# Attention in a four-stage kernel: mask products shared by four heads, three probability buffers, the next queries turned in two parts

## The chip, the cores and the metric

The kernel runs on one core of a Trainium2 chip as one program. The metric is the device time of one execution in microseconds. Each core has TensorE (PE, matrix products), VectorE (DVE), ScalarE (ACT), GpSimd (POOL) and SyncE (SP), which here only issues DMAs. Every engine works its instructions off in order and waits on semaphores.

## The reference, cut to what matters

Input `x` and context `ctx_2048` are 8 batches of 256 rows of 512 float32 numbers. Two layers follow, each a gated cross-attention and a gated feed-forward part. The change touches the first attention:

```python
x = x + tanh(g_xattn[0]) * _L0_xattn_ref(_layernorm(x), ctx_2048, mask_SxS2, mask_BxS2, Wq, bq, Wk, bk, Wv, bv, Wo, bo)

# _L0_xattn_ref: H = 32 query heads of HD = 16, G = 8 key/value groups, 4 query heads share a group
q = X @ Wq.T + bq; k = enc @ Wk.T + bk; v = enc @ Wv.T + bv
scores = einsum('bgrqd,bgkd->bgrqk', q, k) / sqrt(16)
scores = where(causal_mask, -inf, scores); scores = where(padding_mask, -inf, scores)
out = einsum('bgrqk,bgkd->bgrqd', softmax(scores), v) @ Wo.T + bo
```

The "causal" mask is one 256 x 256 mask for all heads and batches; the padding mask is one row per batch. Everything is float32; the kernel keeps float32 accuracy with products of float16 high and low parts.

## The kernel before, in words

The kernel has four phases in one program. Phase A is the first attention, phase B the first feed-forward part with ternary weights, phase C the second attention, phase D the second feed-forward part with routing. Phase A is a software pipeline over the batches b = 0 to 7, written out by hand: each engine has a function `body(b, ...)` of NS = 32 steps, and the order of its instructions is the order of these steps. A step n of batch b holds

- `turned_scores(b, n)` on PE: the scores with keys on the partitions, for two heads at once, 512 columns (L748, L750), into one of two banks;
- ScalarE: two exponentials of that bank, one in float16 (`ph`, L1031) and one in float32 (`prob`, L1032);
- POOL: `pl = prob - ph` (L1143), the low half of the probability. `prob` has 2 buffers, `ph` and `pl` have NP = 4;
- `times_v(b, n - LAG)` on PE, LAG = 3 steps later: 12 narrow products with the values (L767, L769, L771);
- `scores(b + 1, n)` on PE: the scores of the next batch with queries on the partitions (L727, L730), of which VectorE takes the row maxima (L1232).

The maxima are needed before the exponentials. They are negated, turned by PE (`turn_maxima`, L738), copied by ScalarE (`take_maxima`, L957) and written by DMA (`place_maxima`, L549) into a spare row of the turned queries `qT`, so that `turned_scores` subtracts them.

A head takes 64 of the 128 rows of a product. A chunk of `qT` stacks two heads (2i, 2i+1). A chain of products goes over these two heads in the same bank: first `half == 0`, a mask product (identity times the added mask, 512 columns, L727 and L748) and the key chunk [k; 0], which gives head 2i. When the bank has been read, `half == 1` adds the key chunk [-k; k], which turns the scores of head 2i into those of head 2i+1. So there is one mask product for every two products of the chain, in steps with n % 4 in (0, 1), and 16 chunks of queries per batch. The queries come into `qT` by DMA transposes from SP (`place_q`, L559), 8 per batch; the keys by PE transposes (`turn_k`, L713) and VectorE copies (L1225).

Other work is spread over the steps: the projections of batch b + 2 (`q_of` in steps 15 to 18 and 21 to 24, `kv_of` in 19, 20, 25 and 26; ScalarE and VectorE take their results in `high_q` L934, `low_q` L1206, `high_kv`, `low_kv`), the output projection of batch b - 1 (transposes L780 in steps 5 and 6, products in steps 7 to 14), the last normalisation of batch b - 1 on VectorE (`normalise`, L1248 and L1251, step 3), the layer-norm moments of batch b + 3 on VectorE (`moments`, L1177 to L1183, step 4, for b up to 4), the normalisation on ScalarE (`normal`, L970, steps 11 and 13), and on POOL the cut of context and input of batch b + 3 into halves (`FRONT`; L1076, L1080 for the context, L1087, L1091 for the input). Context and input go through the same buffers `fbuf` and `fcut`: `normal` writes `fbuf` and first waits for both low halves of the context (`c_lo`). SP loads and places all of these in its own order of the steps.

In batches 4 to 7 the weights of phase B are made ternary on the side: VectorE scales and rounds a piece (`magnitude`, L1194), ScalarE takes its sign (`sign`, L996), SP turns it by DMA. Batch 7 has 14 such pieces, in steps 1, 3, ..., 27, and no scores of a next batch.

Before body 0 stands a stretch in which the scores of batch 0 (32 steps), the projections of batches 0 and 1 and the first transposes are done; there batch 0's queries are turned by PE (`turn_q`, L701).

```python
    LAG = 3
    PQ, PK = (15, 21), (19, 25)
    NEG0, NEG1 = 27, 4
    NORM = LAG + 8
    def which(m):
        u = m % 16
        return u // 8, 4 * (m // 16) + 2 * (u // 4 % 2) + u % 2, u // 2 % 2
```

Of the kernel before, what the change touches and what calls it, by code (L numbers as in the profile page):

```python
# [60 lines left out]
def flamingo(nc, a, out, phases="ABCD"):  # L61
    with ExitStack() as ctx:
# [204 lines left out]
        with nc.Block() as block:  # L267
# [5 lines left out]
            @block.gpsimd  # L273
            def _(pool):
                of_a[1](pool)
                of_b[1](pool)
# [11 lines left out]
            @block.vector  # L288
            def _(dve):
                low_output, residual = of_a[4](dve)  # L290
                of_b[4](dve, low_output, residual)
# [44 lines left out]
def phase_a(nc, a, env):  # L336
# [8 lines left out]
    def sb(name, shape, dt=F32):  # L345
# [5 lines left out]
    XTh = sb("a_xTh", [P, KC, 2, 2 * P], F16)  # L351
    XTl = sb("a_xTl", [P, KC, 2, 2 * P], F16)
# [6 lines left out]
    qk = sb("a_qk", [P, 2, 2, H0 // 2, S], F16)  # L359
    qT, kT = qk[:, :, 0], qk[:, :, 1]  # L360
# [32 lines left out]
    brow = sb("a_brow", [1, NB])  # L393
    blow = sb("a_blow", [1, NB], F16)
# [7 lines left out]
    mx = sb("a_mx", [P, 2, 2, 2, H0 // 4])  # L402
# [7 lines left out]
    on = sb("a_on", [P, 2, 2, D])  # L410
# [4 lines left out]
             "lk0", "lk1", "hv0", "hv1", "lv0", "lv1", "tq", "tq0", "tq1", "tk", "cq", "ck", "S", "M", "nm",  # L415
             "nt", "nc", "ng0", "ng1", "ST", "E", "L", "AV", "ON", "To0", "To1", "hO0", "hO1", "lO0", "lO1", "O0", "O1", "x0", "x1", "ch")
# [6 lines left out]
    o_hi, o_lo, o_tp = (sem("o_" + n) for n in ("hi", "lo", "turned"))  # L423
    n_ch, n_var, n_rstd, n_nm, n_nrm, n_half = (sem("n_" + n) for n in (
        "chain", "var", "rstd", "nmean", "normed", "half"))
# [6 lines left out]
    t_tp = [sem(f"t_turned{i}") for i in range(2)]  # L432

    NS = 2 * G0 * 2
    LAG = 3
# [8 lines left out]
    NEG0, NEG1 = 27, 4  # L444
# [10 lines left out]
    NPIECE = 32  # L455
    ROUND = 12582912.0
    SUM_AT = [1, 5, 9, 13, 17, 21, 25, 29]
    CUT_AT = [1, 6, 11, 17, 23, 28]
    WO_AT = [12, 14, 16, 18]
# [20 lines left out]
    def cut_piece(b, n):  # L480
# [3 lines left out]
        if b == 7 and n in LAST_AT:  # L484
            return 18 + LAST_AT.index(n)

# [21 lines left out]

    def on_sp(sp):
# [8 lines left out]
        def place_ctx(f):  # L518
            if f >= 2:
                sp.wait_ge(ev["KV1"], f - 1)  # L520
            for t in range(2):
# [4 lines left out]
            for t in range(2):  # L526
# [4 lines left out]
        def place_x(f):  # L531
            if f >= 2:
                sp.wait_ge(ev["Q1"], f - 1)
            for t in range(2):
                sp.wait_ge(x_lo, 2 * (f - 1) + t + 1)
                cols = slice(t * P, (t + 1) * P)
                sp.dma_start_transpose(XTh[:, :, f % 2, cols], fcut[:, t, 0, :]).then_inc(x_tp[f % 2], 16)
                sp.dma_start_transpose(XTl[:, :, f % 2, cols], fcut[:, t, 1, :]).then_inc(x_tp[f % 2], 16)

        def load_piece(l):  # L540
            if l >= NST:
# [2305 lines left out]
```

## Time and profile before

| | us |
|---|---|
| median of 3 runs (lowest, highest) | 1677.6 (1674.11, 1680.73) |
| the profiled execution | 1674.66 |
| its span | 1672.9 |
| PE, DVE, ACT, POOL busy in the span | 1577.2, 972.7, 709.0, 824.7 |
| mean granted TensorE clock | 0.984 |

The span goes from the first to the last instruction of the profiled execution. Busy times of PE are those of overlapping products whose ends are modelled. Body 0 starts at 78.5 us, body 1 at 130.4, body 5 at 340.0, body 6 at 390.7 and body 7 at 441.3 (the first L750 of each); the attention's last exponential is at 491.6.

### The profile page before, as it was taken

The page shows a single profiled execution, that of the slowest core. Times are in us where ns is not written, and L with a number is a line of the kernel's source. Part 1 is how long each engine was busy: PE and PEld are TensorE (multiplying, and loading weights), DVE is VectorE, ACT ScalarE, POOL GpSimd, SP SyncE. Part 2 cuts the span into 40 slices and gives each one's busy share as a digit, 9 for nine tenths or more (in the row PEclk, how much of TensorE's full clock was granted, in tenths as well). Part 3 has the DMA queues.
Part 4 walks back from the last instruction along what each step waited for, and adds up shares of the span by engine and source line. Part 5 has one row for each costly group of instructions (what it writes and reads, how often), then busy time and mean ns, then how long its engine had stood idle before and what let it go on. Part 6 is the DMA issues. An engine that isn't in the chain of part 4 may idle for free. (4 is left out here: it accounts for less than half of the span.)

```text
span 1672.9 us, 29168 instructions
## 1 busy us (share of the span) xinstructions
PE 1577.2 (94%) x10826; PEld 825.8 (49%) x10826; DVE 972.7 (58%) x1947; ACT 709.0 (42%) x1311; POOL 824.7 (49%) x853
## 2 busy tenths in 40 slices
PE   5889999999789999999999989999999999999998
PEld 3446665566444444445556544444444444444443
DVE  5756766778748999845665643377454333322246
ACT  3288888888885655523232321211111111133321
POOL 3488887877874445533452435444342442022234
PEclk9899999999889999999999999999999999999999
DMA  6654545323354554444454436456553755288855
GB/s 187 168 121 96 121 91 115 93 68 75 83 118 101 108 122 98 90 82 86 97 121 95 76 75 152 117 118 141 93 120 79 151 123 107 77 191 192 190 151 189
DMA packets 453954, 195.66 MB, mean 117 GB/s; under 512 B 395500, under 2 KB 418286, under 8 KB 453816
## 3 DMA queue, kind: packets, MB, share of 16 engines
q1 hardware_dynamic: 440216, 171.26, 46.3%
q0 software_dynamic: 5680, 18.62, 4.4%
q10 hardware_dynamic: 7920, 3.93, 1.0%
q8 instruction: 88, 1.44, 0.4%
q14 instruction: 50, 0.41, 0.1%
HBM read 77.17 MB, written 22.81 MB: 60 GB/s over the span
## 5 line engine op out<-in xcount | busy, mean ns | idle before, releaser
L1143 POOL TENSOR_TENSOR a_pl<-a_prob,a_ph 128x512 f16<-128x512 f32 x256 | 295.2, 1165 | 75.3 <-ACT a_prob L1032 74.9
L1232 DVE TENSOR_REDUCE a_mx<-bank 128x2 f32<-128x512 f32 x256 | 173.3, 686 | 86.8 <-PE bank L730 85.3
L140 PE MATMUL bank<-XTh,d_whs 128*128 128x512 f16 x512 | 194.8, 380 | 3.9 <-PEq L89 2.4
L142 PE MATMUL bank<-XTh,d_wls 128*128 128x512 f16 x512 | 194.8, 380 | 0.0
L141 PE MATMUL bank<-XTl,d_whs 128*128 128x512 f16 x512 | 194.6, 380 | 0.0
L1031 ACT ACTIVATE a_ph<-bank 128x512 f16<-128x512 f32 x256 | 153.9, 601 | 59.9 <-PE bank L750 36.6
L2431 POOL CAST d_cut<-d_raw 128x512 f16<-128x512 f32 x90 | 57.6, 640 | 226.8 <-DMA d_raw<-in_L_ffn_sw 145.8
L1032 ACT ACTIVATE a_prob<-bank 128x512 f32<-128x512 f32 x256 | 154.3, 603 | 0.0
L2351 DVE TENSOR_TENSOR d_hid<-d_hid,bank 128x512 f32<-128x512 f32 x64 | 43.9, 686 | 170.8 <-PE bank L142 166.9
L2342 ACT ACTIVATE d_hid<-bank 128x512 f32<-128x512 f32 x64 | 38.2, 597 | 205.5 <-PE bank L142 205.5
L2346 ACT ACTIVATE d_hh<-d_hid 128x512 f16<-128x512 f32 x64 | 40.3, 629 | 193.6 <-DVE d_hid L2351 193.6
L1533 PE MATMUL bank<-b_wpj,b_hTh 128*128 128x512 f16 x256 | 98.1, 383 | 13.2 <-DMA b_hTl<-b_hcut 13.1
L2443 POOL DMA_INDIRECT e_x<-rows,d_who x39 | 37.5, 963 | 147.1 <-DMA e_xTl<-e_x 141.1
L2433 POOL TENSOR_TENSOR d_cut<-d_raw,d_cut 128x512 f16<-128x512 f32 x90 | 106.3, 1181 | 7.2
L767 PE MATMUL bank<-a_v,a_ph 128*128 128x17 f16 x1024 | 103.3, 172 | 4.7 <-POOL a_pl L1143 4.6
L730 PE MATMUL bank<-a_qk 128*128 128x256 f16 x512 | 99.9, 279 | 7.8 <-DVE a_mx L1232 7.7
L750 PE MATMUL bank<-a_qk 128*128 128x512 f16 x256 | 100.7, 393 | 6.4 <-ACT a_prob L1032 6.3
L2361 DVE SCALAR_TENSOR_TENSOR X<-bank,tg,X 128x512 f32<-128x512 f32 x112 | 76.3, 745 | 50.3 <-PE bank L142 50.3
L767 PEld LDWEIGHTS bank<-a_v,a_ph 128*128 128x128 f16 x1024 | 88.6, 97 | 28.4 <-POOL a_pl L1143 7.1
L771 PE MATMUL bank<-a_v,a_pl 128*128 128x17 f16 x1024 | 102.0, 171 | 0.0
L769 PE MATMUL bank<-a_v,a_ph 128*128 128x16 f16 x1024 | 101.9, 170 | 0.0
L769 PEld LDWEIGHTS bank<-a_v,a_ph 128*128 128x128 f16 x1024 | 84.2, 97 | 29.5 <-issue 3.0
(348 smaller groups left out, 4005.0 us busy)
## 6 DMA issues: line engine op xcount, KB each, us to landing
d_raw<-in_L_ffn_w SPq DMA_DIRECT2D x48, 256.0 KB, 3.0
d_raw<-in_L_ffn_sw SPq DMA_DIRECT2D x42, 256.0 KB, 3.1
made<-e_y SPq DMA_DIRECT2D x39, 256.0 KB
a_stage<-in_L_ffn_w_fc SPq DMA_DIRECT2D x32, 256.0 KB, 2.9
a_stage<-in_L_ffn_w_proj SPq DMA_DIRECT2D x32, 256.0 KB, 3.0
a_fbuf<-in_ctx SPq DMA_DIRECT2D x16, 256.0 KB, 3.3
rows<-f_cut SPq DMA_DIRECT2D x16, 256.0 KB, 2.5
out_x<-X SPq DMA_DIRECT2D x16, 256.0 KB, 2.5
```

Of the source, the lines that this page charges most:

```text
L140: nc.tensor.matmul(out_ap, lhi, rhi, start=first, stop=False)
L141: nc.tensor.matmul(out_ap, lhi, rlo, start=False, stop=False)
L142: return nc.tensor.matmul(out_ap, llo, rhi, start=False, stop=last_one)
L750: nc.tensor.matmul(bk[:, :], kT[:, par, 2 * g + half, kc * P:(kc + 1) * P], qT[:, par, 2 * g:2 * g + 2, :].rearrange("p r q -> p (r q)"), ...
L767: nc.tensor.matmul(into[:, c:c + HD0 + 1], ph[:, n % NP, q], vv[:, b % 3, kc, g, 0:HD0 + 1], start=first, stop=False, skip_group_check=True)
L769: nc.tensor.matmul(into[:, c:c + HD0], ph[:, n % NP, q], vv[:, b % 3, kc, g, HD0 + 1:VW], start=False, stop=False, skip_group_check=True)
L771: last = nc.tensor.matmul(into[:, c:c + HD0 + 1], pl[:, n % NP, q], vv[:, b % 3, kc, g, 0:HD0 + 1], start=False, stop=(kc == 1), skip_grou ...
L1031: nc.scalar.activation(ph[:, n % NP, :], bank[BST + n % 2][:, :], ACT.Exp)
L1032: nc.scalar.activation(prob[:, n % 2, :], bank[BST + n % 2][:, :], ACT.Exp).then_inc(ev["E"], 1)
L1143: nc.gpsimd.tensor_tensor(pl[:, n % NP, :], prob[:, n % 2, :], ph[:, n % NP, :], ALU.subtract).then_inc(ev["L"], 1)
L1232: nc.vector.tensor_reduce(mx[:, h, tt, half, 2 * (g % 4):2 * (g % 4) + 2], bank[BS + m % 2][:, :].rearrange("p (r k) -> p r k", r=2), AX_X ...
L2433: nc.gpsimd.tensor_tensor(cut[:, i % RING, 1, :], raw[:, i % RING, :], cut[:, i % RING, 0, :], ALU.subtract).then_inc(p_lo, 1)
```

## The change

- The chain of products now goes over four heads: one mask product for the first, then each further product turns the scores of one head into those of the next. This needs a query chunk for each pair of neighbours, 30 chunks instead of 16, and two heads of one product now belong to groups g and g + 4, so a turned product of 512 columns becomes two of 256.
- Hence 16 DMA transposes of queries per batch instead of 8 (`place_q`), those of the first two tiles issued apart (`tts`), and three transfers of maxima instead of two. Batch 0's second half and batch 1's first half of the chunks are turned by PE and copied by ScalarE before body 0 (`turn_early`, `take_early`).
- `prob` has NR = 3 buffers, `ph` and `pl` NP = 5; LAG is 4. To make room, `on` and the turned input have one buffer.
- The maxima of the next batch's first half are turned in step 20 (NEG0), between the two query projections, and no longer in 27.
- POOL's cuts of context and input move two to three steps later, SP places the context in two parts (steps 8 and 12) and the input in step 28; VectorE's moments move from step 4 to 3, the last normalisation of the batch before from step 3 to 4 (it stands at LAG).
- In batch 7 VectorE does every fourth subtraction `prob - ph` in place of POOL, and 7 of the 14 signs in place of ScalarE, each as two clamps.
- Semaphores of some chains are merged.

```diff
-    qk = sb("a_qk", [P, 2, 2, H0 // 2, S], F16)
+    NC = 30
+    qk = sb("a_qk", [P, 2, NC + 2 * G0, S], F16)
-    NP = 4
-    prob = sb("a_prob", [P, 2, D])
+    NP, NR = 5, 3
+    prob = sb("a_prob", [P, NR, D])
-    LAG = 3
+    LAG = 4
-    NEG0, NEG1 = 27, 4
+    NEG0, NEG1 = 20, 4
-    WO_AT = [12, 14, 16, 18]
+    WO_AT = [9, 14]
...
     def which(m):
-        u = m % 16
-        return u // 8, 4 * (m // 16) + 2 * (u // 4 % 2) + u % 2, u // 2 % 2
+        return m % 2, m // 16, m // 2 % 8
+    def key_chunk(h, r, j):
+        first = j == 0 or j == 4
+        return 8 * h + 4 * r + 2 * (j // 4) + (0 if first else 1)
+    def query_chunk(h, r, j):
+        if j % 2:
+            return 16 * h + j - 1 + r
+        return 16 * h + j + r if j % 4 == 0 else 16 * h + 8 + j - 2 + r
+    def on_dve_low(b, n):
+        return b == B - 1 and n % 4 == 3
+    def on_dve_cut(i):
+        return i >= LATE and i % 2 == 1
...
-        def place_q(b, h):
-            if b >= 2:
+        def place_q(b, h, tts=range(2)):
+            if b >= 2 and tts[0] == 0:
                 sp.wait_ge(ev["ST"], NS * (b - 2) + 16 * (h + 1))
-            for tt in range(2):
+            for tt in tts:
                 sp.wait_ge(ev[f"lq{tt}"], b + 1)
-                for u in range(2):
-                    p0 = 8 * h + 4 * u
-                    sp.dma_start_transpose(qT[:, b % 2, p0:p0 + 4, tt * P:(tt + 1) * P],
+                for r in range(2):
+                    h0, to = 8 * h + 16 * r, 16 * h + r
+                    sp.dma_start_transpose(qT[:, b % 2, to:to + 7:2, tt * P:(tt + 1) * P],
...
+                    n = 3 if h else 4
+                    sp.dma_start_transpose(qT[:, b % 2, to + 8:to + 7 + 2 * n:2, tt * P:(tt + 1) * P],
...
-                if b + 2 < B and n == PQ[1] + KC + 1:
-                    place_q(b + 2, 0)
+                for tt in range(2):
+                    if b + 2 < B and n == PQ[tt] + KC + 1 + tt:
+                        place_q(b + 2, 0, [tt])
-                if f < B and n == 10:
-                    place_ctx(f)
+                if f < B and n in (8, 12):
+                    place_ctx(f, [n // 12])
-                if f < B and n == 22:
+                if f < B and n == NS - 4:
                     place_x(f)
...
         def turned_scores(b, par, n):
-            if half == 0:
+            if n % 8 < 2:
                 nc.tensor.matmul(bk[:, :].rearrange("p (r k) -> p r k", r=2), ident16[:, :],
                                  maddT[:, kc, :].unsqueeze(1).broadcast_to([P, 2, S]), start=True, stop=True)
-            nc.tensor.matmul(bk[:, :], kT[:, par, 2 * g + half, kc * P:(kc + 1) * P],
-                             qT[:, par, 2 * g:2 * g + 2, :].rearrange("p r q -> p (r q)"),
+            for r in range(2):
+                last = nc.tensor.matmul(bk[:, r * S:(r + 1) * S], kT[:, par, key_chunk(h, r, j), kc * P:(kc + 1) * P],
+                                        qT[:, par, query_chunk(h, r, j), :], start=False, stop=True,
...
+        def turn_early(b, h, tt, i):
+            n = 4 * b + 2 * i + tt
+            if n >= 2:
+                pe.wait_ge(ev["cm"], n - 1)
+            for j in range(6 if h and i else 8):
+                h0 = 16 * (j % 2) + 2 * (j // 2) + i + 8 * h
+                c = qs[:, tt, h0:h0 + 2, :].rearrange("p h c -> p (h c)")
+                last = nc.tensor.transpose(bank16(BAV + n % 2)[:, j * P:(j + 1) * P], c, ident16[:, :])
+            last.then_inc(ev["tm"], 1)
...
                 if more and n == NEG0:
                     if more2:
-                        wait("lq1", b + 2)
+                        wait("lq0", b + 2)
                     turn_maxima(b + 1, 0)
...
-        FRONT = {2: (ctx_high, 0), 4: (ctx_low, 0), 7: (ctx_high, 1), 9: (ctx_low, 1),
-                 14: (x_high, 0), 16: (x_low, 0), 19: (x_high, 1), 21: (x_low, 1)}
+        FRONT = {4: (ctx_high, 0), 6: (ctx_low, 0), 9: (ctx_high, 1), 11: (ctx_low, 1),
+                 17: (x_high, 0), 19: (x_low, 0), 22: (x_high, 1), 24: (x_low, 1)}
...
+        def clamp(i):
+            x = stage[:, (NPIECE + i) % NST, :]
+            dve.wait_ge(t_mag, i + 1)
+            nlink(nc.vector.tensor_scalar(x, x, ROUND, 1.0, ALU.subtract, ALU.min))
+            dve.wait_ge(t_tp[i % 2], 16 * (i // 2))
+            nc.vector.tensor_scalar(tern[:, i % 2, :], x, -1.0, None, ALU.max).then_inc(t_dve, 1)
...
-                if b and n == 3:
+                if b and n == LAG:
                     normalise(old[0], b - 1, G0 // 2 - 1)
-                if b + 3 < B and n == 4:
+                if b + 3 < B and n == 3:
                     moments(b + 3)
```

## Rows read from the trace of the kernel before

**Rows 1.** The page's first line.
```profile
span 1672.9 us, 29168 instructions
```

**Rows 2.** Busy us by body: stretch, length, PE, PEld, DVE, ACT, POOL; clock; DMA share; GB/s.
```profile
78.50:130.40 51.90, 45.76 (x564) 27.02 (x563) 30.83 (x59) 42.94 (x94) 42.05 (x40) 0.97 0.54 115
130.40:182.30 51.90, 49.68 (x635) 31.73 (x634) 34.51 (x65) 43.74 (x97) 43.29 (x42) 1.00 0.55 104
...
340.00:390.70 50.70, 49.46 (x635) 31.72 (x634) 36.41 (x65) 42.10 (x85) 37.05 (x33) 1.00 0.28 70
390.70:441.30 50.60, 43.39 (x568) 26.71 (x567) 43.14 (x84) 41.29 (x79) 42.51 (x41) 0.93 0.29 69
441.30:490.30 49.00, 41.13 (x488) 21.79 (x487) 30.36 (x56) 44.00 (x84) 42.49 (x40) 0.87 0.51 114
```
**Rows 3.** Groups of PE instructions in bodies 1 to 4: busy, mean ns | idle before.
```profile
L748 PE MATMUL bank<-a_maddT,ident 128*128 128x512 f16 x65 | 24.8, 382 | 1.4 <-DMA a_qk<-a_nT 0.9 <-ACT a_prob L1032 0.3
L727 PE MATMUL bank<-a_madd,ident 128*128 128x512 f16 x64 | 24.1, 376 | 0.0
```

**Rows 4.** Waits in bodies 1 to 4: total us, times, longest.
```profile
ACT a_ph L1031 <- POOL a_pl L1143: 9.4, 18, 1.8
```

**Rows 5.** Timeline of PE, steps 19 and 20 of body 1: start, us, instruction.
```profile
160.72 0.39 PE L750 MATMUL bank<-a_qk 128*128 128x512 f16 x1
...
162.86 0.38 PE L727 MATMUL bank<-a_madd,ident 128*128 128x512 f16 x1
163.07 0.38 PE L730 MATMUL bank<-a_qk 128*128 128x256 f16 x2
163.29 0.27 PE L140 MATMUL bank<-a_wkvh,a_cTh 128*128 128x256 f16 x1
```

**Rows 6.** Timelines of ACT and DVE, the first queries of body 1.
```profile
162.12 1.03 ACT L934 ACTIVATE a_qs<-bank 128x1024 f16<-128x1024 f32 x1
...
163.18 0.69 DVE L1206 SCALAR_TENSOR_TENSOR a_qs<-bank,a_qs 128x512 f16<-128x512 f32 x1 [0.82 <-ACT a_qs L934]
```

**Rows 7.** Timeline of DVE, steps 3 to 5 of body 1.
```profile
134.49 0.25 DVE L1248 RECIPROCAL a_rec<-bank 128x16 f32<-128x16 f32 x1
...
135.71 0.68 DVE L1225 COPY a_qk<-bank 128x1024 f16<-128x1024 f16 x1
136.31 1.28 DVE L1177 BATCH_NORM_STATS2 a_stats<-X 128x6 f32<-128x512 f32 x2
...
138.86 1.27 DVE L1232 TENSOR_REDUCE a_mx<-bank 128x2 f32<-128x512 f32 x2
```

**Rows 8.** Timeline of PE, step 6 of body 1 and the start of step 7.
```profile
139.60 0.39 PE L730 MATMUL bank<-a_qk 128*128 128x256 f16 x2 [0.81 <-DVE a_mx L1232]
139.82 0.60 PE L780 MATMUL bank<-ident,a_on 128*128 128x128 f32 x4
140.26 0.38 PE L750 MATMUL bank<-a_qk 128*128 128x512 f16 x1
```

**Rows 9.** Timelines of POOL and ACT, steps 8 to 11 of body 1.
```profile
144.54 2.28 POOL L1143 TENSOR_TENSOR a_pl<-a_prob,a_ph 128x512 f16<-128x512 f32 x2
146.77 1.17 POOL L1080 TENSOR_TENSOR a_fcut<-a_fbuf,a_fcut 128x512 f16<-128x512 f32 x1
...
148.47 0.81 ACT L970 ACTIVATE a_fbuf<-X,a_nmean,a_rstd 128x512 f32<-128x512 f32 x1
```

**Rows 10.** Timeline of PE, step 28 of body 1.
```profile
178.12 0.61 PE L713 MATMUL bank<-ident,a_ks 128*128 128x128 f16 x8 [1.13 <-DVE a_v L1218]
```

**Rows 11.** Timeline of SP's issues at the end of body 1.
```profile
174.09 5.12 SPq L559 DMA_TRANSPOSE a_qk<-a_qs  x4
179.25 1.36 SPq L549 DMA_DIRECT2D a_qk<-a_nT  x2
180.92 0.33 SPq L543 DMA_DIRECT2D a_stage<-in_L_ffn_w_proj  x1
181.29 1.44 SPq L516 DMA_DIRECT2D a_fbuf<-in_ctx  x2
```

**Rows 12.** The scaling of pieces, line L1194: min/median/max ns.
```profile
L1194 DVE TENSOR_SCALAR a_stage<-a_stage,b_scale x32: 470/913/1458, 289.9 to 485.1; 128x512 f32<-128x512 f32 x32
```

**Rows 13.** Groups of ACT instructions in body 7: the signs.
```profile
L996 ACT ACTIVATE a_tern<-a_stage,a_unround 128x512 f16<-128x512 f32 x14 | 10.2, 730 | 1.9 <-DMA b_wpj<-a_tern 1.3 <-DVE a_stage L1194 0.6
```

**Rows 14.** Timeline of PE before body 0, step 20 of batch 0's scores.
```profile
65.53 0.61 PE L727 MATMUL bank<-a_madd,ident 128*128 128x512 f16 x1 [1.88 <-DVE a_mx L1232]
```

More of the change, by code:

```diff
@@ L422, in phase_a @@
     w_in, o_in, g_tr, g_hi, g_lo = (sem("g_" + n) for n in ("in", "wo_in", "tr", "hi", "lo"))
-    o_hi, o_lo, o_tp = (sem("o_" + n) for n in ("hi", "lo", "turned"))
+    o_lo, o_tp = (sem("o_" + n) for n in ("lo", "turned"))
     n_ch, n_var, n_rstd, n_nm, n_nrm, n_half = (sem("n_" + n) for n in (
-        "chain", "var", "rstd", "nmean", "normed", "half"))
+        "chain", "var", "rstd", "nmean", "normed", "pool_chain"))
     c_hi, c_lo, c_wr, x_hi, x_lo = (sem("n_" + n) for n in ("chi", "clo", "cwritten", "xhi", "xlo"))
@@ L516, in load_ctx, with place_ctx @@
                 sp.dma_start(fbuf[:, t, :], ctx_tiles[:, 2 * f + t, :]).then_inc(c_in[t], 16)
-        def place_ctx(f):
-            if f >= 2:
+        def place_ctx(f, ts=range(2)):
+            if f >= 2 and ts[0] == 0:
                 sp.wait_ge(ev["KV1"], f - 1)
-            for t in range(2):
+            for t in ts:
                 sp.wait_ge(c_lo, 2 * f + t + 1)
@@ L525, in place_ctx @@
                 sp.dma_start_transpose(CTl[:, :, f % 2, cols], fcut[:, t, 1, :]).then_inc(c_tp[f % 2], 16)
-            for t in range(2):
+            for t in ts:
                 rows = slice((2 * f + t) * P, (2 * f + t + 1) * P)
@@ L666, in q_of @@
                 pass
+            elif tt and b >= 2:
+                wait("nc", b - 1, 1, 2)
             elif tt:
@@ L716, in scores @@
         def scores(b, par, m):
-            tt, g, half = which(m)
-            bk = bank[BS + m % 2]
+            tt, h, j = which(m)
+            bk = bank[BS + tt]
             wait("M", b, m + 1, NS)
@@ L741, in turned_scores @@
         def turned_scores(b, par, n):
-            g, half, kc = n // 4, n // 2 % 2, n % 2
-            bk = bank[BST + n % 2]
+            kc, h, j = which(n)
+            bk = bank[BST + kc]
             wait("E", b, n + 1, NS)
             if n % 16 == 0:
-                wait(f"ng{n // 16}", b, 32, 32)
-            if half == 0:
+                pe.wait_ge(ev[f"ng{h}"], 48 * (b + 1))
+            if n % 8 < 2:
                 nc.tensor.matmul(bk[:, :].rearrange("p (r k) -> p r k", r=2), ident16[:, :],
@@ L754, in times_v @@
+            last.then_inc(ev["ST"], 1)
         def times_v(b, n):
-            g, half, kc = n // 4, n // 2 % 2, n % 2
+            p, j, kc = n // 8, n // 2 % 4, n % 2
             if n % 8 == 0:
-                wait("ON", b, g // 2 + 1, G0 // 2)
-            wait("L", b, n + 3, NS)
-            into = bank[BAV + g // 2 % 2]
+                wait("ON", b, p + 1, G0 // 2)
+            low_done(pe, b, n)
+            into = bank[BAV + p % 2]
             for r in range(2):
+                g = p + 4 * r
@@ L1017, in on_act @@
         high_kv(0, 1)
+        for i in range(2):
+            for tt in range(2):
+                take_early(0, 1, tt, i)
         for tt in range(2):
@@ L1021, in on_act @@
         take_maxima(0, 0)
+        for i in range(2):
+            for tt in range(2):
+                take_early(1, 0, tt, i)
         normal(2, 0)
@@ L1444, in phase_b @@
     b_ctx = sem("b_context")
-    b_mh, b_ch, f_var, f_rs, f_nm, f_xn, f_cl, f_hi, f_lo = (sem("bf_" + n) for n in (
-        "half", "chain", "var", "rstd", "nmean", "normed", "clipped", "hi", "lo"))
+    f_var, f_rs, f_nm, f_xn, f_cl, f_hi, f_lo = (sem("bf_" + n) for n in (
+        "var", "rstd", "nmean", "normed", "clipped", "hi", "lo"))
     f_tp = [sem(f"bf_turned{i}") for i in range(LEAD)]
```

231 lines of the change are left out of this document (142 added, 89 removed).

## The prediction

> **What bounds the kernel now.** I read the span and the profiled run's time first, then the busy times by batch, the PE groups and waits of batches 1 to 4, and last the engines' timelines at the few places where the change moves something. The profiled execution spans 1672.9 us [rows 1] and took 1674.66 us, 2.9 under the median of the three runs (1677.6). The attention loop is body 0 to 7, 32 steps each, from 78.5 to about 493 us. The edit touches that loop and the stretch before it; what follows starts when it ends, so I carry a difference there to the end unchanged. Bodies 1 and 5 take 51.9 and 50.7 us with PE busy 49.7 and 49.5; POOL is at 43.3 in the first, which also cuts the next context and input [rows 2]. In bodies 6 and 7 PE drops to 43.4 and 41.1 and no engine is full. So PE's order bounds bodies 1 to 5, with POOL close behind, and in 6 and 7 latencies between four engines do.
>
> **The masks.** PE spends 64 + 64 mask products of 512 columns in bodies 1 to 4 [rows 3]. Their 0.38 us is latency; they follow each other 0.22 apart (162.86 to 163.07) [rows 5]. A mask per four heads instead of two removes 8 + 8 of them per batch, 3.5 us of PE, from steps 4, 5, 12, 13, 20, 21, 28 and 29. Over eight batches that is 128 x 0.216 = 27.6 us, and this is what the edit seems to promise. I take each pair of steps by itself, for batches 1 to 4.
>
> Steps 4 and 5 (0.86 us less). VectorE's block of moments stands at step 4: two statistics and a last small operation, 136.31 to 138.86, or 2.55 us [rows 7]. PE waits 0.8 for the maximum behind it, at 139.60 [rows 8]. The edit puts the block at step 3, still ahead of that step's maximum, and puts the normalisation of the batch before (134.49 to 135.1 today) at step 4, behind it, because the lag grows to 4. From the batch's start (130.4) I count: third maximum ends at 4.1, block to 6.7, maximum and key copy to 7.9, normalisation (one more product, so 0.85) to 8.8. PE's output transposes of step 5 wait for it (0.44, as those from 139.82 to 140.26), then comes step 6 with 1.2: step 7 starts at 10.5, where it now starts at 9.9 [rows 8]. (Step 5's maximum, too, is late, but less.) The 0.86 is gone and 0.6 is added. Bounds: 0.9 won to 1.5 lost.
>
> Steps 12 and 13 (0.86 less). ScalarE writes the normalised input over the context's buffer at step 11, and waits for the second low half of the cut. That half is at POOL's step 9 now and ended at 147.94, before ScalarE came to it at 148.47 [rows 9]. The edit puts it at POOL's step 11, behind that step's subtraction, which itself needs ScalarE's exponential of step 11. From the end of that exponential ScalarE waits 1.12 + 1.12, then 0.7 for the normalisation and 1.1 for the next exponentials. Two score banks let PE go on to step 13 and it stops at 14. A step with a projection takes it 1.4 without masks, so step 14 would come 4.2 after step 11, which is 2.6 after the end of exponential 11; the wait, the normalisation and exponential 12 take 4.1. So 1.5 are lost. The third probability buffer doesn't help, for it is the producer that stands. Bounds: none (if POOL were not behind) to 2.5. What is queued behind the wait: ScalarE's exponentials, then PE's step 14, VectorE's maxima and POOL's subtractions.
>
> Steps 20 and 21 (0.86 less). The turned maxima move from step 27 to 20 and wait for the low half of the first queries. ScalarE took these at 162.12, VectorE ended at 163.87 [rows 6]; PE's step 19 began at 160.72 and its step 20 reached the place at 163.29 [rows 5], 162.86 without the two masks. So PE waits 1.0 with the key projection queued behind, and pays the 0.2 of the transposes here. Net 0.4 lost. Bounds 0.2 to 1.2.
>
> Steps 28 and 29 (0.86 less). At 28 PE waits 1.1 for the value's low half before the key transposes [rows 10]; that chain starts with step 27's exponential, so a mask less only lengthens the wait, but ScalarE's copy of the maxima no longer stands in it (0.26). I give 0.5 here, 0.2 at step 29 and 0.2 for the start of the next batch, where the maxima now come early.
>
> Sum for one of batches 1 to 4, against today: 0.6 lost by step 7; 1.5 - 0.9 = 0.6 lost by step 14; 0.4 lost at 20 and 21; 0.9 won at the end. That is +0.7 us, 3.0 for the four; bounds -6 to +8. ScalarE's waits for POOL there, 9.4 us over four batches [rows 4], are what the third buffer removes; PE is hardly held by them, so I count nothing.
>
> Batch 5 has no moments, no context and no input: three pairs of masks won (2.6), 1.2 lost at step 20, 0.9 won at the end, makes -2.3 (bounds -3.5 to -1). Batch 0 has POOL in front for twenty steps (42.1 busy of 51.9, of which it idles in the start [rows 2]); the later input cut removes a wait for the context's writes and the wait of step 11 takes as much: 0 (bounds -3 to +2). Batch 6 has VectorE at 43.1 of 50.6 and PE with slack: half of 3.5 at most, -1.5 (-3 to 0).
>
> **The other PE work.** One turned product of 512 columns becomes two of 256. Two 256-column products take 0.38 together and the next starts 0.22 after the first [rows 5]: the second weight load hides; nothing (up to 0.03 each, 7 us, if it did not). Before the loop 60 transposes are added and 4 DMA transposes leave; PE stands 1.9 us for VectorE in that stretch [rows 14], and ScalarE is idle, so they are covered; the first scores wait for one more round of copies, 0.7, less some masks: +0.5 (-2 to +3).
>
> **SP.** Four query transposes take it 5.1 us [rows 11]; there are 16 instead of 8 per batch from batch 2 on, and three maxima transfers instead of two: 10 + 1.4 us more. Today a batch has 16 transposes at 1.28 and some 20 transfers at 0.3 to 0.7, together 31 us of 52; so it has room, but not at the start of a batch: the input's four transposes move to step 28, the context's load (181.29 today) goes out 3 us later against the batch, and POOL needs it at step 4. I get a landing near 7.5 against a need at 7.9: nothing, to 2 us per batch if late.
>
> **Batch 7.** ScalarE is busy 44.0 of 49.0 [rows 2] and loses 7 of 14 signs of 0.73 [rows 13], 5.1 us. POOL loses 8 subtractions of 1.14 [rows 9]. VectorE, 30.4 busy, takes them: 14 operations like the scaling, 0.9 [rows 12], and 8 priced like its maxima of that size, 0.64 (1.27 for two [rows 7]; up to 1.8 if each first waits for a POOL operation): 18 us, so 48 us, as long as the batch. They come in bursts (magnitude, two clamps, a subtraction, 3.3 us at every fourth step), and ScalarE's next sign waits for a magnitude behind them. Such a scaling takes 0.47 to 1.46 us here [rows 12]. The Trainium skill (SBUF — State Buffer, "SBUF: two separate sides") says that a VectorE operation in a two-port mode or with two SBUF inputs and a GpSimd operation exclude each other for a whole instruction. The spread agrees; by that rule each moved subtraction too could wait up to 1.2 us, and the batch would come out some 3 us over my sum. Without it: the work that ends last today (the last pieces' loads) hides part of the burst. I take -0.5 (bounds -3 to +5).
>
> **Sum.** +3.0 - 2.3 + 0 - 1.5 + 0.5 - 0.5 = -0.8 us: 1673.9 against the profiled 1674.66, and 1676.8 against the median. The bounds lean a little to the fast side (the third buffer and the longer lag are counted at nothing), so I say 1676.
>
> **The rivals.**
> The masks come through (25 in 100). If POOL runs less far behind and the moments hide, batches 1 to 4 win 2.2 each, batch 0 2, batch 5 2.3, batch 6 2.5 and batch 7 3 with ScalarE lighter: -18, or 1660. For it: PE's high share in bodies 1 to 5. Against it: each of the three waits follows from the order of the instructions and from durations in the rows.
> SP's queue decides (17 in 100), the other side. Place: the first steps of bodies 0 to 4. If the boundary's ten transposes run at the slower pace that some show, the context lands 2 us or more after POOL's step 4; POOL idles over 8 us of a batch [rows 2], but not there, where its operations follow each other without a gap [rows 9]; so it passes the delay on to step 11 and to ScalarE: 2 to 3 us in each of five batches, +12, or 1689. It decides from a landing later than about 8 us into the batch.
> The second weight load shows (6 in 100): 256 x 0.03 = 7 us and the sum above, 1684. Against it are the 256-column pairs.
> My forecast, no change, has 52 in 100; its own range is 1670 to 1684.
>
> A measurement of this kernel tells 0.5%, 8.4 us, from no change. Faster by more: the first rival and a little of the forecast's fast side, 0.29. Slower by more: the second, part of the third and the forecast's slow side, 0.21. Within: 0.50. The range 1662 to 1687 leaves about 10 in 100 on either side.
>
> **What would show it.** In the changed kernel's trace: 64 + 64 masks instead of 128 + 128 (else the edit isn't what it says); in bodies 1 to 4 ScalarE idle some 2.3 us before its first normalisation, with the context's low half as releaser; PE idle about 1.0 at step 20 before the maxima's transposes, and VectorE's normalisation ahead of PE's output transposes; VectorE over 44 us busy in body 7. I am wrong if bodies 1 to 4 take under 50 us, or if ScalarE shows no such wait, or if POOL waits for the context's load.

## The result

The changed kernel takes 1689.7 us (median of 7 runs, 1685.5 to 1696.2), the one before 1677.6 (7 runs beside it). The ratio is 1.0073, 95% interval [1.0056, 1.0090]: 12 us slower. The forecast was 1676, no change within 0.5%, and its range ended at 1687. The profiled execution took 1685.5, the fastest of the seven and 4.3 under their median, and spans 10.8 us more than that of before [rows 1].

The page's first line, then busy us by body, in the columns of [rows 2]:

```profile
span 1683.7 us, 29655 instructions
```

```profile
75.90:129.70 53.80, 42.98 (x568) 30.28 (x567) 32.38 (x61) 42.72 (x94) 41.72 (x40) 0.90 0.62 114
129.70:183.90 54.20, 46.76 (x651) 33.15 (x650) 35.69 (x70) 43.61 (x97) 43.54 (x42) 1.00 0.58 118
...
294.80:352.80 58.00, 51.36 (x652) 35.35 (x651) 40.54 (x78) 42.79 (x86) 42.41 (x41) 0.91 0.51 109
352.80:405.20 52.40, 47.97 (x652) 34.05 (x651) 37.70 (x69) 41.40 (x85) 36.99 (x33) 0.97 0.46 95
405.20:454.20 49.00, 40.62 (x583) 28.15 (x582) 44.23 (x87) 40.85 (x79) 42.11 (x40) 0.93 0.41 80
454.20:504.00 49.80, 38.81 (x522) 24.58 (x521) 43.07 (x81) 39.47 (x78) 36.75 (x33) 0.86 0.45 111
```

The reader is to see the column behind POOL: the granted clock of TensorE. It was 1.00 in all of bodies 1 to 5 before ([rows 2] has 1 and 5); in bodies 1, 4 and 5 it is now 1.00, 0.91 and 0.97. TensorE is busy 46.8 us in body 1 instead of 49.7, and the body is 2.3 us longer all the same. By term of the forecast, in us of the profiled executions:

| stretch | forecast | measured |
|---|---|---|
| up to body 0 | +0.5 | -2.7 |
| body 0 | 0 | +2.0 |
| bodies 1 to 4 | +3.0 | +13.5 (2.3, 2.5, 2.6, 6.1) |
| body 5 | -2.3 | +1.6 |
| body 6 | -1.5 | -1.5 |
| body 7 | -0.5 | +0.4 |
| behind the loop | 0 | -2.5 |

The last row says little: no experiment below edits what follows the loop, and yet it took 1180.1 us (changed) to 1187.9 us (e7) in the profiled executions, and 1182.6 in that of before.

What TensorE waits for in bodies 1 to 4 (total us, times, longest):

```profile
PE bank L782 <- DVE a_v L1319: 6.6, 4, 1.7
PE bank L822 <- ACT a_prob L1127: 5.8, 4, 1.5
PE bank L801 <- DVE a_mx L1333: 4.5, 5, 1.1
PE bank L854 <- DVE a_on L1354: 3.9, 4, 1.0
PE bank L809 <- DVE a_qs L1307: 3.6, 4, 0.9
...
PE bank L798 <- DMA a_qk<-a_qs: 0.9, 1, 0.9
```

There is about one of each kind per body: L822 is step 14 behind ScalarE, L854 the output transposes behind the normalisation, L809 the maxima's transposes at step 20 behind the queries' low half, L801 the maximum behind the moments, L782 the key transposes of step 28 (four waits of at most 1.13, 4.4 in all, before [rows 10]).

To see where the time went I took the trace of TensorE apart, product by product, over bodies 0 to 5: **work** is what each product takes at full clock with the next right behind it (0.216 us for 512 columns, 0.108 for 256), **half clock** is what the products in stretches with a granted clock of 0.5 (1.2 instead of 2.4 GHz) take over that, **standing** the rest. A wait that falls into a stretch at half clock can be put to either of the last two columns; that leaves 1 us or so open between them.

| bodies 0 to 5, us | length | work | standing | half clock |
|---|---|---|---|---|
| before | 312.2 | 275.5 | 35.1 | 1.4 |
| changed | 329.3 | 254.6 | 62.9 | 11.8 |
| e4, masks back | 327.8 | 275.5 | 48.3 | 4.0 |
| e5, three edits | 309.6 | 254.6 | 44.8 | 10.0 |
| e12, e5 with masks | 314.2 | 275.3 | 35.9 | 2.7 |
| e13, before, cuts later | 315.6 | 275.5 | 36.4 | 3.6 |
| e11, five edits | 301.9 | 254.6 | 42.3 | 5.1 |

The change took 20.9 us of work out and put 27.8 us of standing and 10.4 us of half clock in. These are single executions; the granted clock over the whole run, as the median of all runs, says the same: 0.974 changed against 0.984 before (0.979 and 0.984 in the two profiled ones). What one fall looks like, in body 4: windows around steps 13 to 15 (columns as above), and TensorE's wait ahead of it.

```profile
313.00:319.00 6.00, 5.87 (x77) 3.61 (x74) 4.41 (x9) 3.29 (x6) 4.80 (x5) 1.00 0.36 88
319.50:322.00 2.50, 1.68 (x20) 0.99 (x20) 0.69 (x1) 2.50 (x6) 1.66 (x2) 1.00 0.61 155
322.10:325.50 3.40, 3.40 (x25) 1.90 (x25) 2.48 (x3) 1.79 (x4) 2.78 (x3) 0.50 0.67 164
325.60:331.00 5.40, 5.40 (x75) 3.42 (x72) 3.20 (x4) 3.89 (x8) 3.52 (x4) 1.00 0.44 115
```

```profile
320.32 0.39 PE L822 MATMUL bank<-a_qk 128*128 128x256 f16 x2 [1.46 <-ACT a_prob L1127]
...
322.13 0.61 PE L822 MATMUL bank<-a_qk 128*128 128x256 f16 x2
```

TensorE stood at 319 to 320, and from 322 it is "busy" all the time at a clock of 0.50; the same pair of products takes 0.61 instead of 0.39, and step 15 takes 2.85 us where body 1's takes 1.67.

### The profile page after: what moved, and what is told of

It reads as the page before. It is cut to its first block and busy times, and to the rows that moved or that the text cites. A ratio compares the mean times of both kernels' runs of the same rounds, so it can differ in the third digit from the quotient of the medians.

```text
span 1683.7 us, 29655 instructions
## 1 busy us (share of the span) xinstructions
PE 1560.7 (93%) x11014; PEld 846.0 (50%) x11014; DVE 994.8 (59%) x2001; ACT 709.5 (42%) x1312; POOL 817.0 (49%) x845
## 5 line engine op out<-in xcount | busy, mean ns | idle before, releaser
L1237 POOL TENSOR_TENSOR a_pl<-a_prob,a_ph 128x512 f16<-128x512 f32 x248 | 286.7, 1170 | 96.5 <-ACT a_prob L1127 95.7
L822 PE MATMUL bank<-a_qk 128*128 128x256 f16 x512 | 105.0, 289 | 18.7 <-ACT a_prob L1127 18.2
L801 PE MATMUL bank<-a_qk 128*128 128x256 f16 x512 | 100.7, 280 | 15.3 <-DVE a_mx L1333 14.9
L1645 PE MATMUL bank<-b_wpj,b_hTl 128*128 128x512 f16 x256 | 98.0, 383 | 0.0
L140 PE MATMUL bank<-d_whd,d_hh 128*128 128x512 f16 x256 | 97.1, 379 | 1.1 <-DVE d_hl L2463 1.1
```

Source lines behind the costliest of these rows:

```text
L140: nc.tensor.matmul(out_ap, lhi, rhi, start=first, stop=False)
L822: last = nc.tensor.matmul(bk[:, r * S:(r + 1) * S], kT[:, par, key_chunk(h, r, j), kc * P:(kc + 1) * P], qT[:, par, query_chunk(h, r, j), ...
L1237: nc.gpsimd.tensor_tensor(pl[:, ring(b, n, NP), :], prob[:, ring(b, n, NR), :], ph[:, ring(b, n, NP), :], ALU.subtract).then_inc(ev["L"], 1)
```

## The experiments

All runs beside the kernel before on the same chip; a ratio is against it. 0.1% is 1.7 us.

| run | median us | ratio, 95% | granted clock, median of its runs |
|---|---|---|---|
| before | 1677.3 to 1678.9 | 1 | 0.984 |
| changed | 1689.7 | 1.0073 [1.0056, 1.0090] | 0.974 |
| e1 moments behind | 1690.6 | 1.0068 [1.0047, 1.0090] | 0.972 |
| e2 input later | 1681.5 | 1.0020 [0.9999, 1.0042] | 0.976 |
| e3 maxima behind | 1686.0 | 1.0035 [1.0022, 1.0047] | 0.972 |
| e4 masks back | 1689.6 | 1.0056 [1.0038, 1.0075] | 0.983 |
| e5 three edits | 1669.7 | 0.9954 [0.9936, 0.9972] | 0.978 |
| e6 body 7 as before | 1689.8 | 1.0062 [1.0039, 1.0085] | 0.974 |
| e7 two buffers | 1687.9 | 1.0058 [1.0039, 1.0076] | 0.973 |
| e8 queries later | 1691.3 | 1.0073 [1.0055, 1.0092] | 0.975 |
| e9 e5, maxima direct | 1665.1 | 0.9927 [0.9905, 0.9950] | 0.980 |
| e10 e5, keys later | 1667.4 | 0.9937 [0.9921, 0.9954] | 0.980 |
| e11 five edits | 1660.8 | 0.9895 [0.9878, 0.9912] | 0.982 |
| e12 e5 with masks | 1678.1 | 0.9998 [0.9979, 1.0017] | 0.984 |
| e13 before, cuts later | 1681.2 | 1.0023 [1.0005, 1.0042] | 0.981 |
| e14 e11, moments split | 1664.1 | 0.9923 [0.9898, 0.9948] | 0.979 |

**e1.** The moments go behind the normalisation.

```
-                if b + 3 < B and n == 3:
+                if b + 3 < B and n == LAG:
                     moments(b + 3)
```

> VectorE's block of moments goes from step 3 back to step 4, behind the normalisation of the batch before. Theory (the waits at fixed places make the loss): the 1.15 us that TensorE stands before the output transposes of step 5 in bodies 1 to 4 goes, the wait for the maximum (1.2) stays near 0.95, so bodies 1 to 4 get 1.0 to 1.3 us shorter each, some 5 us in all, and up to 2 more where a fall of the clock behind step 5 goes too: 1683 to 1686 us against 1689.7. Rival (SP's queue and the DMA transposes make the loss): the wait moves to another release, bodies 1 to 4 change by less than 0.4 each, time 1689 to 1691.

No gain that can be told, so the theory's number is wrong, and the time is in the rival's range. TensorE's wait for ScalarE in bodies 1 to 4, ScalarE's for POOL in bodies 1 to 3, and POOL's for the context in body 1:

```profile
PE bank L822 <- ACT a_prob L1127: 7.1, 4, 2.1
```

```profile
ACT a_fbuf L1059 <- POOL a_fcut L1174: 8.6, 3, 3.1
```

```profile
140.12 0.61 POOL L1170 CAST a_fcut<-a_fbuf 128x512 f16<-128x512 f32 x1 [1.01 <-DMA a_fbuf<-in_ctx]
```

The wait L854 is gone (3.9 in the changed kernel), and L822 grew by 1.3: ScalarE stands 8.6 instead of 7.3 for POOL's cut in the same three bodies. Body 1 wins 1.06 at steps 5 and 6 and loses 0.68 at 13. There TensorE comes earlier, but POOL doesn't: it waits 1.01 for the context's load, for which it didn't wait in body 1 of the changed kernel, and then works without a gap until the cut ends at 151.96. The waits stand in series on one chain, and in body 1 the load, which SP issues, is part of it; so the rival isn't refuted here, though bodies 2 to 4 change by +0.1, -0.7 and -1.9 (most of the last is clock) where it gave less than 0.4. Its share wasn't taken apart.

**e2.** ScalarE normalises the input at steps 14 and 16.

```
-                if b + 3 < B and n in (11, 13):
-                    normal(b + 3, (n - 11) // 2)
+                if b + 3 < B and n in (14, 16):
+                    normal(b + 3, (n - 14) // 2)
```

> ScalarE normalises the input at steps 14 and 16 instead of 11 and 13; POOL's order stays. Theory of the waits: ScalarE no longer stands 2.3 us behind exponential 11 for the context's second low half, TensorE's 1.6 us before step 14 in bodies 1 to 4 and its 4.9 us in body 0 go, and with the latter most of the half clock behind it (about 3 us). Bodies 1 to 4 1.3 to 1.7 shorter each, body 0 5 to 8 shorter: 10 to 14 us in all, 1676 to 1680 us. Rival (SP's queue): POOL's and SP's work only come later, the loss stays, under 4 us won. A third outcome between them: in body 0 POOL is so far behind that the exponentials wait for its subtractions instead, then body 0 wins under 3 and the sum is 7 to 9.

9 us by the ratios, the largest single effect, just short of the 10 to 14 expected. It is the number of the third outcome (7 to 9, body 0 under 3 shorter: 51.9 instead of 53.8), but what stands in body 0 is not what that outcome names. Body 1's step 13 takes 1.38 instead of 3.00. In body 0 the 4.8 us at step 14 are gone, but step 18 takes 4.77 instead of 1.80, behind one small operation of VectorE:

```profile
98.47 6.02 DVE L1340 TENSOR_SCALAR a_nmx<-a_mx 128x32 f16<-128x32 f32 x1
104.42 0.68 DVE L1333 TENSOR_REDUCE a_mx<-bank 128x2 f32<-128x512 f32 x1
```

```profile
96.61 1.16 POOL L1174 TENSOR_TENSOR a_fcut<-a_fbuf,a_fcut 128x512 f16<-128x512 f32 x1
97.73 6.73 POOL L1237 TENSOR_TENSOR a_pl<-a_prob,a_ph 128x512 f16<-128x512 f32 x6
106.10 0.61 POOL L1181 CAST a_fcut<-a_fbuf 128x512 f16<-128x512 f32 x1 [1.64 <-DMA ctx_lo<-a_fcut]
```

POOL's six subtractions follow each other without a gap and end at 104.46; VectorE's scaling of 32 columns, which takes 0.18 at its fastest, ends at 104.49. e9 tests it.

**e3.** The maxima's transposes go behind the two key projections of step 20.

```
+                    if tt and n == NEG0:
+                        wait("lq0", b + 2)
+                        turn_maxima(b + 1, 0)
...
```

(Left out: the same lines ahead of the projections go, except for batches without a batch b + 2.)

> The transposes of the maxima stay at step 20 but stand behind the two key projections of that step instead of ahead of them. Theory of the waits: the 1.06 us that TensorE stands for the queries' low half in bodies 0 to 5 is covered by the projections (6 products, 1.3 us); the second query projection at step 21 now waits for ScalarE's copy of the maxima, up to 0.5. So 0.5 to 1.1 per body, six bodies, 3 to 6.5 us: 1683 to 1687 us. Rival (this wait only moves to the next release of the same chain): each body under 0.3 shorter, 1688 to 1690 us.

6.4 us by the ratios, as expected: step 20 of body 1 takes 2.01 instead of 2.99, and only 0.2 is left of the wait.

**e4.** The removed masks are issued again (shown for the scores; the turned scores alike).

```
+            if m % 8 in (4, 5):
+                nc.tensor.matmul(bk[:, :].rearrange("p (r k) -> p r k", r=2), ident16[:, :],
+                                 madd[:, tt, :].unsqueeze(1).broadcast_to([P, 2, S]), start=False, stop=True,
+                                 skip_group_check=True)
```

> The 128 mask products of 512 columns that the change removed are issued again, added to the same banks at steps 4, 5, 12, 13, 20, 21, 28 and 29; the masks are then added twice. Everything else is the changed kernel. Theory of the waits: they stand where TensorE waits for others anyway, at 4, 5, 12, 13, 20 and 28 they are covered in bodies 1 to 4, at 21 and 29 they cost 0.43 each; with bodies 5 to 7 open in part that is 8 to 12 us of the 27.6 that 128 x 0.216 would be: 1698 to 1702 us. Rival (the gain of the masks came through in full and something else ate it, such as the second weight load of the split products): 25 to 28 us, 1715 to 1718 us.

Both were wrong: 128 products cost nothing (1.0056 against 1.0073; the intervals leave room for 2 us at most). In the table above they take 14.6 us of standing and 7.8 us of half clock away in bodies 0 to 5. Bodies 1 to 5 of the kernel with them, and of the changed one:

```profile
130.40:404.30 273.90, 253.04 (x3334) 174.84 (x3333) 186.90 (x356) 217.52 (x459) 211.52 (x197) 0.99 0.51 111
```

```profile
129.70:405.20 275.50, 242.57 (x3254) 171.18 (x3253) 185.82 (x356) 216.03 (x459) 211.73 (x197) 0.96 0.53 111
```

More work, the same time, a clock of 0.99 instead of 0.96. What the rival asked about also falls: the split products cost nothing, a step without waits takes the same in the kernel before and in the changed one (step 8 of body 1: 1.82 and 1.82, step 9: 1.60 and 1.60).

**e5.** e1, e2 and e3 together.

> The edits of the three runs before it together: moments behind the normalisation, input normalised at steps 14 and 16, maxima behind the key projections. Alone they were worth 0 (1690.6), 8 (1681.5) and 4 us (1686.0) against 1689.7. Theory (waits in series): the 1.05 us that the moments gained at step 5 were given back at ScalarE's wait of step 12, because POOL's chain came later; with that wait gone they count. So 8 + 4 + 4 = 16 us, 1672 to 1676. Rival (the loop is bound by something common to all, such as POOL's sum of work or SP's queue, and each wait removed only shows the next): no more than the best edit alone, 1678 to 1682.

20 us by the ratios, where the three alone make 16 (0.05%, 0.53%, 0.38%). The intervals of these sums are wider than the 4 us between them, so the times don't show that the moments now count. Body 1 of the trace does: steps 5 and 6 take 3.67 instead of 4.74, and step 13 takes 1.39, as in e2, and gives nothing back. The kernel is faster than the one before.

**e12.** The masks of e4 in the kernel of e5.

> The kernel of the three edits with the 128 removed mask products issued again (the masks are then added twice). In the changed kernel they cost nothing (1689.6 against 1689.7), because waits of TensorE and the stretches at half clock shrank by as much. Theory: with the waits of steps 12, 13 and 20 gone, those at 12, 13, 20, 21 and 29 now count, 2.1 us in each of bodies 1 to 5, 3 in bodies 6 and 7, less some 3 us that the clock gives back: 8 to 12 us, 1678 to 1682, as long as the kernel before. Rival (TensorE's work never counts in this loop, the chains of the other engines set it): within 3 us, 1669 to 1673.

The masks now cost 7.4 us (0.9998 against 0.9954), about as expected, and the kernel with them is as fast as the one before: the whole gain of e5 over it is the masks. Of the 27.6 us that 128 x 0.216 seem to promise, 0 arrives in the changed kernel and 7.4 in e5.

**e13.** In the kernel before, only POOL's order.

```
-        FRONT = {2: (ctx_high, 0), 4: (ctx_low, 0), 7: (ctx_high, 1), 9: (ctx_low, 1),
+        FRONT = {4: (ctx_high, 0), 6: (ctx_low, 0), 9: (ctx_high, 1), 11: (ctx_low, 1),
```

> The kernel before, with one thing of the change: POOL cuts the next context at steps 4, 6, 9 and 11 instead of 2, 4, 7 and 9. All masks, two probability buffers, moments, maxima and SP's order are those of the kernel before. Theory (this order alone makes the loss of step 11): ScalarE stands 2 us or more behind exponential 11 of bodies 0 to 4, TensorE stops at step 14; the masks of steps 12 and 13 hide under it. Bodies 1 to 4 0.5 to 1.5 us longer, body 0 3 to 5, and some stretches at half clock where there were none, 1 to 4: 1683 to 1689 us against 1678. Rival (the wait comes of the change as a whole, the lag of 4 steps or the third buffer): within 2 us of the kernel before, 1676 to 1680.

The wait comes of this order alone, in all four bodies:

```profile
ACT a_fbuf L970 <- POOL a_fcut L1080: 8.8, 4, 2.4
```

(9.2, 4, 2.4 in the changed kernel.) It costs 0.76 in body 1, close to the 0.6 that the prediction gave it, and 3.8 us in all, between the theory's 5 to 11 and the rival's 2. Half clock came in body 0 alone (2.2 us more in the table above); bodies 1 to 5 keep 1.00. So this wait, with all masks in place, doesn't bring the clock down there.

Nor is it needed: e5 is free of it and has half clock in four of bodies 1 to 5. All sixteen traces fall into two groups. In bodies 1 to 5, TensorE runs at a granted clock of 0.50 for 0, 0, 0 and 3.4 us in the four kernels with all masks (before, e13, e12, e4), and for 4 to 35 us in the twelve without: 4 to 17 where the edits of e1 to e3 are all in, 14 to 35 elsewhere. So the lighter work is what the falls have in common, and there are mostly more of them where more waits stand; which wait starts a given fall isn't shown.

**e6.** POOL and ScalarE take all of batch 7 again (`on_dve_low` returns False, `LATE = 32`).

> Batch 7 as before the change: POOL does all 32 subtractions, ScalarE all 14 signs, VectorE none. Theory: the bursts on VectorE at steps 19 to 23 (clamps of 1.27 and 1.26, a subtraction of 1.63) make TensorE stand 6.7 us there, but the last steps then run faster, so body 7 changes by less than 1 us: 1688 to 1691 us. Rival (the moved work is the loss of body 7 and beyond): body 7 is 2 to 3 us shorter, 1686 to 1688. Other rival (it was a gain that the masks don't show): body 7 2 us or more longer, over 1692.

The time is as expected, its reason isn't: body 7 is 3.9 us shorter (45.5), and the stretch behind it 6 longer in this execution, which is less than that stretch varies between the kernels' executions. The bursts are there in the changed kernel:

```profile
487.76 1.27 DVE L1294 TENSOR_SCALAR a_stage<-a_stage 128x512 f32<-128x512 f32 x1
489.06 1.26 DVE L1296 TENSOR_SCALAR a_tern<-a_stage 128x512 f16<-128x512 f32 x1
490.24 1.63 DVE L1491 TENSOR_TENSOR a_pl<-a_prob,a_ph 128x512 f16<-128x512 f32 x1
...
493.39 0.43 DVE L1294 TENSOR_SCALAR a_stage<-a_stage 128x512 f32<-128x512 f32 x1
```

1.27 beside POOL, 0.43 with POOL idle. Whether something takes body 7's gain back behind the loop can't be told: the interval of the ratio is wider than the gain.

**e7.** `NP, NR = 5, 2`.

> Two probability buffers instead of three in the changed kernel (ScalarE's exponential waits for POOL's subtraction of two steps before). The prediction counted the third buffer at nothing. By that: ScalarE again idles some 9 us for POOL over bodies 1 to 4, bodies 1 to 5 each within 0.5 us, time 1689 to 1692. Rival (the third buffer carries the kernel): bodies 0 to 5 each 1 to 2 us longer, 1696 to 1702.

The third buffer is worth nothing here, as the prediction had it: ScalarE idles 9.7 us for POOL again in bodies 1 to 4, and TensorE loses nothing by it; bodies 0 to 5 differ by up to 3 us either way, most of it clock (body 4: 4.0 us of it and 1.3).

**e8.** SP issues half of the next queries' transposes at step 7.

```
-                    place_q(b + 1, 1)
+                    place_q(b + 1, 1, [0])
+                if b + 1 < B and n == 7:
+                    place_q(b + 1, 1, [1])
```

> SP issues the second two tiles' four transposes of the next queries at step 7 instead of step 0 of each batch, behind the ternary pieces of steps 1 and 6. Theory: SP's queue makes a loss only in body 5, where the transpose of the ternary piece goes out at 369.99 us behind eight query transposes and lands at 372.37, so that ScalarE stands 3.1 us and TensorE 2.2; that goes, the other bodies stay within 0.4: 1687 to 1688 us. Rival (SP's queue decides in bodies 0 to 4 too): these get 1 us or more shorter each, 1683 or less; or, if the queries then come too late for step 16, a wait there and longer bodies, 1692 or more.

What it removes is this, in body 5 of the changed kernel: SP's issues, and ScalarE waiting for one of them.

```profile
368.68 1.26 SPq L614 DMA_TRANSPOSE a_qk<-a_qs  x1
369.99 1.27 SPq L632 DMA_TRANSPOSE b_wfc<-a_tern  x1
```

```profile
372.45 0.72 ACT L1085 ACTIVATE a_tern<-a_stage,a_unround 128x512 f16<-128x512 f32 x1 [3.07 <-DMA b_wfc<-a_tern]
```

Step 13 of body 5 takes 1.38 instead of 3.55, the body 51.3 instead of 52.4. But the time stays at 1.0073, where 2 us less were expected. Bodies 1 to 3 are 1.9, 0.9 and 2.9 us longer in this execution, body 4 is 2.5 shorter, and bodies 1 to 5 have 33.9 us at half clock instead of 20.5. SP's queue is a cause in body 5; in bodies 0 to 4 it shows no gain, though the clock could hide a small one.

**e9.** e5, and the reductions write the maxima in fp16, without the scaling of e2's rows.

```
-                nc.vector.tensor_scalar(nmx[:, h, :, :].rearrange("p t e -> p (t e)"),
-                                        mx[:, h].rearrange("p t e -> p (t e)"), -1.0, None, ALU.mult)\
-                  .then_inc(ev["nm"], 1)
...
```

> The kernel of the three edits, and VectorE's small scaling of the maxima (128x32, nmx from mx) is gone: the reductions write fp16 directly and ScalarE's copy of the turned maxima takes the sign. In body 0 of the two kernels with the later input that scaling takes 6.02 us and ends when POOL's row of operations without a gap ends (102.10 us in both columns), and TensorE stands 4.3 us at step 18. Theory (VectorE's operation waits for a gap of POOL): body 0 gets 2.5 to 4.5 us shorter, the others 0 to 0.5 each: 1663 to 1667 us against 1669.7. Rival (POOL is so far behind in body 0 that something else stands there instead): body 0 within 1 us, 1669 to 1671.

4.5 us by the ratios, as expected but no more than the intervals leave open; the trace has 2.9 of them in body 0 (48.2 instead of 51.1), where step 18 takes 1.80 instead of 4.28.

**e10.** e5 with `TURN0 = 28`.

> The kernel of the three edits, and the key transposes of steps 28 and 30 (with VectorE's copies of them) one step later, 29 and 31. TensorE stands 1.84 us at step 28 for the value's low half of step 27. Theory: step 29's own products (0.75) cover that much, the rest stays, and the copy of step 31 comes late for the next batch's first scores by up to 0.5: 0.3 to 0.9 less per body, six bodies, 2 to 5 us: 1665 to 1668. Rival (the copy's delay at the batch's start takes it all back): 1669 to 1672.

**e11.** e9 and e10, and e8's order for batches 5 to 7 (from body 4 on).

> All of it: the three edits, the maxima written directly, the key transposes one step later, and the second tile's queries of batches 6 and 7 transposed at step 7 (the wait of body 5 for SP's queue). If they add up: 3 to 4 for the maxima, 2 to 5 for the keys, 1 to 2.5 for the queue: 1659 to 1664 us. If they are in series with something common: 1665 to 1670.

e10 wins 2.8 us, inside its range but less than the intervals leave open; e11 is 1.05% faster than the kernel before and 1.8% faster than the changed one. It is the fastest kernel here.

**e14.** e11 with the moments over steps 6 to 8.

> The kernel of the five edits with the block of moments (2.5 us at step 4) dealt over steps 6, 7 and 8, and POOL's deviation and the mean two steps later. Theory: TensorE's 1.1 us for the maximum at step 6 of bodies 1 to 4 goes and nothing follows before step 14, where the input is normalised: 3 to 5 us, 1656 to 1659 us against 1660.8. Rival (as with the moments in the changed kernel: the gain is given back where ScalarE waits for the mean, at step 14): 1660 to 1662.

No gain, so the theory is wrong, and the time is above the rival's range too. Bodies 1 and 2 are 0.8 shorter each, but in bodies 3 and 4 POOL comes to its next cut while the write-back of the last one isn't done, and the exponentials stand behind it:

```profile
311.08 0.61 POOL L1182 CAST a_fcut<-a_fbuf 128x512 f16<-128x512 f32 x1 [6.69 <-DMA ctx_lo<-a_fcut]
```

The next limit there is this write-back (4.0 us in body 3, 6.7 in body 4); whether it is its place in SP's queue or the transfer that is late was not taken apart.

## Why the prediction was wrong

**What held.** Half of the masks are left (33 and 32 in bodies 1 to 4, where there were 65 and 64 [rows 3]). Each of the three waits is there, at its place and of its size: in body 1 ScalarE stands 2.44 at step 11 with the context's low half as releaser (forecast 2.3), TensorE 0.9 ahead of the maxima's transposes (1.0) and 0.98 ahead of the output transposes, for which the normalisation is late (L854). In body 1, against the kernel before, steps 1 to 7 cost +0.4 (forecast +0.6), 12 and 13 +0.8 (+0.6), 20 and 21 +0.4 (+0.4). Body 6, the second weight load (e4's steps without waits) and the third buffer came out as said. And what it said of step 28, "so a mask less only lengthens the wait", e4 shows of nearly all of them.

**The step that failed** is the sum itself. What stands under "Sum for one of batches 1 to 4, against today" adds waits and masks at the full clock that [rows 2] shows for bodies 1 and 5, and has no term for the clock. The row of body 1 with 1.00 stood there beside bodies 6 and 7 with 0.93 and 0.87, where TensorE has slack, so the trace of before did hint at what happens to the clock where TensorE has less to do. The missing term measured +10.4 us in bodies 0 to 5, 6.7 of it in bodies 1 to 4. Two pairs of kernels that differ in the masks alone show it (11.8 against 4.0, 10.0 against 2.7), and e13 shows that the wait of step 11 without the lighter work leaves the clock of bodies 1 to 5 at 1.00. With the clock taken out, bodies 1 to 4 are at +6.8 instead of +3.0; the terms below give some 3 us of the rest. The Trainium skill (TensorE: Matmul & The Clock Gate, "Part 1: The HAM clock gate") tells that a gate passes only a part of TensorE's clock pulses, depending on how busy the engine has been. The rows agree (1.00 beside 0.50), and a forecast for a kernel that loses TensorE's work should have used it.

**Mis-sized terms.** Body 0, forecast 0 because "the wait of step 11 takes as much": POOL is further behind there, and ScalarE waited 3.9 us instead of the 2.4 of body 1, TensorE 4.8:

```profile
91.80 0.59 ACT L1127 ACTIVATE a_prob<-bank 128x512 f32<-128x512 f32 x1
96.28 0.81 ACT L1059 ACTIVATE a_fbuf<-X,a_nmean,a_rstd 128x512 f32<-128x512 f32 x1 [3.89 <-POOL a_fcut L1174]
```

Body 5, forecast -2.3: I counted SP's queue at nothing and looked only at the context's load. The load did come late twice, a sign of being wrong that the prediction named (3.0 us of POOL in bodies 2 and 3), but what counted in body 5 was the piece's transpose behind eight query transposes, 2.2 us. Body 1's start waits 1.0 for a query transpose. The end of a batch: -0.4 instead of -0.9, since TensorE's standing at step 28 grew from 1.29 to 1.84 as step 27 got shorter. Before the loop -2.7 instead of +0.5, below the lower bound of -2; its cause stays open (the granted clock is 0.50 for 17.6 us of that stretch in the trace of before, for 6.8 in the changed one). VectorE in body 7 was 43.1 busy, not over 44, and the body +0.4. Without the moved work it is 3.9 us shorter in e6, which is near the 3 us that the prediction thought possible if each moved subtraction also waits for POOL.

**The rivals.** "SP's queue decides" named 1689, and 1689.7 came, but by another mechanism: its 12 us should come from POOL waiting for the context's load, and POOL waited 3.0 us. The right number there is chance. "The masks come through" fell with e4. "The second weight load shows" fell with the same steps of 1.82 and 1.60 us in both kernels.

## What to carry to other kernels

Work taken from the engine that bounds a loop is worth what its waits don't swallow: put it back as an experiment (e4, e12) before believing its sum. On TensorE price the clock too: it ran at 1.00 where TensorE was nearly full, and here new waits and half clock together cost 38 us against 21 us of work. And waits on one chain hide each other: what a removal wins at one step can be lost at the next wait (e1, body 1) and stay once that wait is gone (e5, body 1), so try them together before dropping one.

## What was not expected of the hardware

A VectorE scaling of 128x32, which takes 0.18 us at its fastest, took 6.02 us in body 0 of e2, e5 and e10 and 5.45 in e12. Each time it ended 0.04 us behind the last of a row of POOL's (GpSimd's) subtractions without a gap. The Trainium skill (SBUF — State Buffer, "SBUF: two separate sides") says of a VectorE operation in a two-port mode or with two SBUF inputs, and one of GpSimd, that the one that starts first holds the shared port for its whole instruction. That alone would make the delay the rest of one instruction, and mostly it is. In e2 too, in body 2:

```profile
181.85 0.96 DVE L1340 TENSOR_SCALAR a_nmx<-a_mx 128x32 f16<-128x32 f32 x1
181.61 3.44 POOL L1237 TENSOR_TENSOR a_pl<-a_prob,a_ph 128x512 f16<-128x512 f32 x3 [0.42 <-ACT a_prob L1127]
```

The scaling ends at 182.81, just behind the first of three subtractions (1.15 us), with the next one already begun. 99 of the 208 scalings in the traces ended like this, after at most 1.2 us. But in the rows of body 0 the waiting operation didn't get its turn at four or five such changes from one subtraction to the next. So the delay can be a whole row instead of one instruction; what decides which of the two comes isn't shown. A small VectorE operation on a critical chain is best folded into one that is there anyway, as e9 does with the reductions.
